# The attention result channel-major through DRAM, with the copies out issued by ScalarE, in a transformer layer on one Trainium2 core

## The reference

```python
# x: (32, 512, 256) float32
def attn(x):                                  # H = 16 heads, hd = 16
    q, k, v = split(x @ w_qkv.T + b_qkv)      # each (B, H, L, hd)
    scores = (q * hd**-0.5) @ k.T + mask      # mask: blocks of 128; block 0 is global
    out = softmax(scores) @ v                 # (B, H, L, hd) -> (B, L, D)
    return out @ w_out.T + b_out
def ffn(x):
    return relu(x @ W1 + b1) @ W2 + b2        # 256 -> 1024 -> 256
x = x + layernorm(attn(layernorm(x)))
x = x + layernorm(ffn(layernorm(x)))
```

## Time and profile before

| quantity | value |
|---|---|
| median of three runs | 2048.34 us |
| the profiled execution, its own time | 2041.29 us |
| its span, first to last instruction | 2039.5 us |
| mean granted clock of TensorE | 0.978 of full speed |
| busy: PE, PEld, DVE, ACT, POOL | 94%, 77%, 74%, 69%, 36% of the span |
| DMA | 160.60 MB, 79 GB/s |

### The profile page before, as it was taken

The page is one execution under the profiler, slowest core; times in us unless marked ns, Lnnn a source line. Parts: engine busy times, 40 slices in busy tenths (PEclk is TensorE's granted clock), DMA queues, the critical chain, the costliest instruction groups (busy, mean ns, idle before and its releaser), DMA issues. The chain is left out here.

```text
span 2039.5 us, 71012 instructions
## 1 busy us (share of the span) xinstructions
PE 1926.4 (94%) x27904; PEld 1575.7 (77%) x27904; DVE 1511.4 (74%) x2913; ACT 1406.0 (69%) x2343; POOL 741.6 (36%) x910
## 2 busy tenths in 40 slices
PE   5789999999999999999999999999999999999985
PEld 3458888777878877888777788787788887778775
DVE  4687777787777778778777777777777777876731
ACT  1457767777776777776677777677777677776763
POOL 3113333334333334433343433333433333343343
PEclk7799999999999999999999999999999999999997
DMA  5333434433333433333343333343334344333200
GB/s 144 74 70 80 89 77 86 85 76 82 81 81 79 93 79 80 79 81 81 82 85 80 79 77 81 80 94 78 77 77 86 76 87 85 78 81 69 56 28 17
DMA packets 132815, 160.60 MB, mean 79 GB/s; under 512 B 29408, under 2 KB 82400, under 8 KB 132576
## 3 DMA queue, kind: packets, MB, share of 16 engines
q1 hardware_dynamic: 130544, 154.13, 35.7%
q10 hardware_dynamic: 2032, 2.69, 0.4%
HBM read 38.21 MB, written 17.83 MB: 27 GB/s over the span
## 5 line engine op out<-in xcount | busy, mean ns | idle before, releaser
L817 DVE TENSOR_REDUCE max_bias<-p_pair 128x4 f32<-128x1024 f32 (+1 forms) x640 | 772.8, 1222 | 262.0 <-PE p_pair L571 139.8
L742 ACT ACTIVATE probs<-p_pair 128x1024 f32<-128x1024 f32 x640 | 634.8, 1026 | 208.4 <-PE p_pair L568 127.6
L964 POOL TENSOR_TENSOR h_lo<-h_f,h_hi 128x512 fp32r<-128x512 f32 x256 | 329.7, 1288 | 507.5 <-ACT h_hi L774 507.5
L571 PE MATMUL p_pair<-stack 49*128 49x256 f32 (+1 forms) x3072 | 319.6, 306 | 39.5 <-DVE max_bias L817 22.7
L774 ACT ACTIVATE h_f<-p_pair,b_s 128x256 f32<-128x256 f32 x512 | 248.8, 486 | 133.1 <-PE p_pair L598 133.1
L571 PEld LDWEIGHTS p_pair<-stack 49*128 49x128 f32 (+1 forms) x3072 | 226.9, 188 | 126.7 <-DVE max_bias L817 59.8
L598 PE MATMUL p_pair<-w_hi,h_hi 64*128 64x256 f32 x2048 | 309.4, 279 | 5.0 <-ACT h_hi L774 2.5
L598 PE MATMUL p_pair<-x_hi,w_hi 64*128 64x256 f32 (+1 forms) x2560 | 302.1, 306 | 9.6 <-DVE x_lo L827 5.2
L598 PE MATMUL p_pair<-w_hi,h_lo 64*128 64x256 f32 x2048 | 305.7, 275 | 0.0
L598 PE MATMUL p_pair<-w_lo,h_hi 64*128 64x256 f32 x2048 | 305.5, 275 | 0.0
L598 PE MATMUL p_pair<-x_hi,w_lo 64*128 64x256 f32 (+1 forms) x2560 | 297.7, 302 | 0.0
(11 more groups left out here) (81 smaller groups left out, 2792.9 us busy)
## 6 DMA issues: line engine op xcount, KB each, us to landing
stack<-qk SPq DMA_DIRECT2D x1536, 64.0 KB, 2.3
xr<-x SPq DMA_DIRECT2D x32, 512.0 KB, 4.2
out<-yf SPq DMA_DIRECT2D x64, 256.0 KB, 2.2
xa<-x SPq DMA_DIRECT2D x31, 512.0 KB, 3.8
shift_rows<-max_t SPq DMA_DIRECT2D x128, 8.0 KB, 1.4
stack<-shift_rows SPq DMA_DIRECT2D x128, 8.0 KB
probs<-w_qkv_t SPq DMA_DIRECT2D x2, 384.0 KB, 5.5
ya<-w ACTq DMA_DIRECT2D x1, 512.0 KB, 8.2
```

The costliest lines, as they stand in the source:

```text
L571: last = nc.tensor.matmul(dst[:, j, col:col + HALF].rearrange("p (a n) -> p a n", a=2), stack[r, stationary, at, kb * P:(kb + 1) * P], two ...
L742: nc.scalar.activation(probs[:, prob_slot(quad, c), :, :], banks("scores", n)[:, :, :], ACT.Exp, scale=SCALE).then_inc(exp_done, 1)
L817: nc.vector.tensor_reduce(dst, src, axis=AX.X, op=ALU.max, negate=True).then_inc(red_done, 1)
L964: nc.gpsimd.tensor_tensor(h_parts[1][:, m:m + 2, :], h_f[:, n % 2, :, :], h_parts[0][:, m:m + 2, :].bitcast(F32), ALU.subtract).then_inc(h ...
```

## The change

The attention result stays channel-major. Steps `o_t` and `o2` are taken out of TensorE's list. In their place:

- `read_o` copies the quad to SBUF as before, into one of two buffers.
- `store_o` (new, ScalarE, once for each quad) issues two DMAs: one moves the four rows of denominators from SBUF to the SBUF tile `den_q` (each row of 512 cut into 32 pieces of 16 elements, 64 bytes), the other writes all 128 partitions of 2 KB to DRAM (`o_rows`, 256 KB).
- SyncE gets six DMAs more for each batch: `load_o` twice (from `o_rows` to `o_ch`, 128 partitions of 2 KB), `store_inv` twice (inverted denominators to DRAM, 16 KB), `load_inv` twice (back, each row read 16 times, 256 KB).
- VectorE takes the reciprocals twice for each batch on a tile of 128 x 32 (`inverse`), multiplies twice on 128 x 512 (`normal_o`) and writes `o2_lo` in two halves; ScalarE writes `o2_hi` in two halves, all from SBUF.
- `o_ch` is the memory of `ya`, the tile of the output projection, so `load_o` waits until the sum of the batch before (`x1_done`) has read `ya`.
- The rows of the output weights are reordered on the host to the new order of channels.
- All tables of the order are written anew, and with them the assignment of PSUM pairs.

```diff
-        ("o_t", 0, -2, 0), ... ("o_t", 3, -2, 1), ... ("o2", 0, -2, 3)       (TensorE: gone)
+        ("exp", 12, -2), ("store_o", 1, -2), ("exp", 13, -2),                (ScalarE)
+        ("load_o", 0, -3), ("load_inv", 0, -3), ("store_inv", 1, -3),        (SyncE)
+        o_t = sb("o_t", [P, 2, L])
+        inv_b = sb("inv_b", [P, KD, L])
+        o_rows = nc.dram_tensor("o_rows", [KD, H // 2, 32, L], F32, kind="Internal").ap()
+        inv_rows = nc.dram_tensor("inv_rows", [KD, H // 2, L], F32, kind="Internal").ap()
+        o_ch = ya[:, :, :].rearrange("p (c a) n -> p c (a n)", c=KD)
...
+                elif what == "load_o":
+                    other, added = count(sp, b, 32, 16 * (n + 1)), count(sp, b, 2, 0)
+                    wait(sp, o_out[0], b, 32, 16 * (n + 1))
+                    reached(sp, o_out[1], other)
+                    reached(sp, x1_done, added)
+                    sp.dma_start(o_ch[:, n, :], o_rows[n, :, 0:HD, :].rearrange("h c n -> c h n")).then_inc(o_in[n], 16)
+                elif what == "store_inv":
+                    rows_free = count(sp, b, 16, 0)
+                    wait(sp, inv_done, b, KD, n + 1)
+                    reached(sp, inv_in[n], rows_free)
+                    sp.dma_start(inv_rows[n].rearrange("(j h) (m t) -> (h m) j t", j=2, t=DT),
+                                 inv_q[:, n, :, :]).then_inc(inv_out[n], 16)
+                elif what == "load_inv":
+                    read = count(sp, b, KD, n + 1 - KD)
+                    wait(sp, inv_out[n], b, 16, 16)
+                    reached(sp, on_done, read)
+                    sp.dma_start(inv_b[:, n, :],
+                                 inv_rows[n].unsqueeze(0).broadcast_to([HD, H // 2, L])).then_inc(inv_in[n], 16)
...
-                elif what == "o2":
-                    wait(pe, ev["o_t"], b, QUADS, QUADS)
-                    last = transposed(dst, lambda r, m: o_n[r, m % KB, m // KB * P:(m // KB + 1) * P], KD * KB)
-                elif what == "o_t":
-                    wait(pe, ot_done, b, QUADS, n + 1)
-                    last = transposed(dst, lambda r, m: o_t[r, m * P:(m + 1) * P], KB)
...
                 elif what == "read_o":
                     wait(act, pv_mm, b, QUADS, n + 1)
-                    wait(act, mm["o_t"], b, QUADS, n)
-                    nc.scalar.activation(o_t[:, :], banks("pv", n)[:, 0, :], ACT.Copy).then_inc(ot_done, 1)
+                    for s in (den_in, o_out):
+                        wait(act, s[n % 2], b, 32, 16 * (n // 2))
+                    nc.scalar.activation(o_t[:, n % 2, :], banks("pv", n)[:, 0, :], ACT.Copy).then_inc(ot_done, 1)
+                elif what == "store_o":
+                    rows_free, den_free = count(act, b, 16, 0), count(act, b, KD, n // 2 + 1 - KD)
+                    wait(act, ot_done, b, QUADS, n + 1)
+                    reached(act, o_in[n // 2], rows_free)
+                    reached(act, inv_done, den_free)
+                    heads = slice(4 * (n % 2), 4 * (n % 2) + 4)
+                    act.dma_start(den_q[:, n // 2, n % 2, :],
+                                 o_t[HD:P:32, n % 2, :].rearrange("h (m t) -> h m t", t=DT)).then_inc(den_in[n % 2], 16)
+                    act.dma_start(o_rows[n // 2, heads].rearrange("h c n -> (h c) n"),
+                                 o_t[:, n % 2, :]).then_inc(o_out[n % 2], 16)
+                elif what == "o2_hi":
+                    wait(act, on_done, b, KD, n + 1)
+                    wait(act, mm["op"], b, 1, 0)
+                    nc.scalar.activation(o2_t[0][:, n, :], o_ch[:, n, :], ACT.Copy).then_inc(hi_done["o2"], 1)
...
+                elif what == "inverse":
+                    for j in range(2):
+                        wait(dve, den_in[j], b, 32, 16 * (n + 1))
+                    wait(dve, inv_out[n], b, 16, 0)
+                    nc.vector.reciprocal(inv_q[:, n, :, :], den_q[:, n, :, :]).then_inc(inv_done, 1)
                 elif what == "normal_o":
-                    (reciprocal of den, two products into o_n, from PSUM)
+                    wait(dve, inv_in[n], b, 16, 16)
+                    wait(dve, o_in[n], b, 16, 16)
+                    nc.vector.tensor_tensor(o_ch[:, n, :], o_ch[:, n, :], inv_b[:, n, :], ALU.mult).then_inc(on_done, 1)
```

539 lines of the change are left out of this document (280 added, 259 removed), and 23 rows, old and new, of tables (LAST, ORDER).

## The result

The changed kernel takes 2126.6 us (median of four runs, 2121.4 to 2129.0), the kernel before 2048.4 in the same runs: the ratio is 1.038, with an interval of 1.035 to 1.040. The profiled execution of the changed kernel took 2129.0 us, its span is 2127.2.

What follows compares the result with a forecast made beforehand. TensorE's list, its steps in a row and short waits for PSUM pairs, was taken as the bound. Per batch -1.1 - 0.7 + 0.5 + 0.2 = -1.1 us, -35 us in 32 batches, plus 2 at the end: 2015 us, range 1984 to 2056.

Steps and rivals of the forecast that it cites:

- (a): TensorE's o_t and o2 transposes go: 1.1 us a batch gained, one o_t not counted because TensorE waits there anyway.
- (b): Five PSUM pair uses a batch go, with the waits behind o_n (0.36 us a batch); counted at nothing.
- (c): Stretch from the last f2 product to quad 3's product on TensorE: 7.6 us against 8.3, a gain of 0.7.
- (d): On TensorE, x1 takes x2's PSUM pair soon after it and waits for x_lo: a loss of 0.5 us.
- (e): ScalarE's eight DMA issues a batch, 0.5 us each, hidden beside TensorE's work: cost nothing, 1.0 us if one pause shows.
- (f): VectorE's swapped steps about even; its waits for DMAs, inverse 0 the tightest, cost 0.2 us a batch, ends 0 and 3.4.
- (g): DMA traffic of 2.1 MB more a batch: DMA engines' share from 0.39 to about 0.55, SyncE's queue has room.
- The ends: Last batch's result goes through DRAM, about 10 us of latency beside the previous batch's feed-forward: 2 us added.
- wrong in kind: Sign: turn shrinks by less than 0.5 us with all transposes gone; then the steps between them set the pace.
- the rivals: ScalarE's pauses reach TensorE, 2077 us, chance 0.14; DRAM chain takes the gain, 2045, 0.18; more than the transposes, 1988, 0.18.

Runs made afterwards that it cites:

- b_few: Kernel before, each o_t step making 2 of its 8 transposes and o2 2 of its 16 (38 fewer a batch); 2063.3 us, ratio 1.009.
- a_fill1: Changed kernel with scores_max 6 to 10 made twice, 16 more products a batch between quads 2 and 3; 2087.9 us, ratio 1.021.
- a_seven: Changed kernel with scores 16 and its exp ahead of quad 2's product, scores_max 9 and 10 behind quad 3's; 2182.1 us, ratio 1.067.
- b_act_dma: Kernel before with eight more DMAs a batch issued by ScalarE, four of 8 KB and four of 256 KB; 2049.0 us, ratio 1.003.
- a_best2: Changed kernel with scores_max 6 to 10 made twice and steps around op reordered on VectorE, SyncE and ScalarE; 2054.3 us, ratio 1.006.
- b_few_but_one: Kernel before with 32 of 48 transposes a batch left out, keeping all eight of o_t 2 between quads 2 and 3; 2043.5 us, ratio 1.000.
- b_traffic: Kernel before with eight more 256 KB DMAs a batch, issued by SyncE behind each load_stack; 2118.2 us, ratio 1.035.

## Why the prediction was wrong

By its own steps, for each batch:

- **(a), transposes, -1.1 us: the mis-sized term, and the step that failed.** It took the transposes' time as free to go and reckoned that the one in the gap was worth nothing, "where TensorE waits anyway". It was worth the clock. Taking it out made the old order 0.6 us a batch slower by the medians and 1.1 by the profiled turns (b_few), and the whole fall cost 1.76 in the new one (a_fill1). What the other transposes bring was too high as well: nothing that can be told for 32 of them, where 0.9 were reckoned. In the new order no run puts back the work of the transposes alone; there the gap is also longer (step c). That their absence is enough rests on b_few and on a_seven.
- **(b), no gain from the pairs:** not tested apart. The wait for `o_n` is gone; those for other readers of pairs came in its place, as the step said.
- **(c), the stretch:** from `f2` to quad 2's product 0.57 us, as said (0.6). From quad 2 to quad 3 5.18 and not 4.69: the copy starts 0.27 us after the product for 0.14 before, the first `exp` 0.71 after the copy's start for 0.49, the fourth `exp` adds 0.92, and TensorE goes on 0.43 after the last for 0.26: 1.44 us more, where 0.95 were taken. With the product of quad 2 that makes 8.04 us for 8.31, a gain of 0.3 and not 0.7. The prediction watched this stretch's length to 0.1 us, and never asked what waiting there does to the product behind it.
- **(d), `x2` and `x1`:** 0.5 us was too dear. The row of `x_lo` is 4.0 us in 25 turns, 0.2 a turn.
- **(e), ScalarE:** 256 issues at 0.556 and 0.502 us, as said; their cost was taken as nothing and measured as 0.24 us a turn with the traffic, in the old order (b_act_dma). Small and inside the bounds.
- **(f), VectorE:** wrong in kind. The two differences of 128x512 were priced at 0.63 us by a copy on ScalarE of that size; alone they take 0.66, beside GpSimd 1.77. The bounds looked at DMA landings, not at the neighbour, and the same rows of before had no such pair. With the waits around it on ScalarE's `relu` and on `h_lo`, this is 61.27 - 60.17 = 1.1 us a turn (a_fill1 against a_best2, by order alone). The order changed on three engines at once, so the 1.1 is not divided between these waits; moving one `o_lo` by itself brought 0.22 to 0.42.
- **(g), traffic:** right. No wait on `stack`, its landing 2.4 us. The DMAs of 256 KB in the detour landed after 3.2 to 3.9 us where 2.2 and 2.3 were taken, that of 16 KB after 1.8, in slack that held.
- **The ends, +2 us:** 17.5. With the clock held and the order mended it is still 14 (a_best2). TensorE's waits for `max_bias` and for `h_lo` rise there in small rows (behind 1800 us that for `h_lo` from 2.3 to 8.0 us in the changed kernel); it was not taken apart further.

The sum against the runs: the prediction had -1.1 us a turn, the profiled executions +2.8, a difference of 3.9 (by the medians the kernel is 78 us slower and not 88, so some 0.3 us of it is scatter). Of it 1.8 us is the clock and 1.1 the place around `op`; each is shown by an edit that takes it away. The other 1.0, the turn of a_best2 against the 59.1 reckoned, is put down to gains of (a) and (c) that never came. For (a) b_few_but_one shows such a shortfall in the old order; how the 1.0 us divides stays open.

The prediction called itself wrong in kind if the turn shrank by less than 0.5 us although all transposes were gone. It grew by 2.8, and the reason given for that case, that the steps between set the pace, leaves the clock out as well. None of the rivals had the clock either. All of them took TensorE's products at one speed. Of the two rules of the Trainium skill that the prediction weighed, the one on busy time (Trainium Kernel Development and Optimization, Performance Expectations) pointed the right way: the share of the weight loads said that there was room, and taking work away brought little. But its measure would not have told of the loss. The other (DMA: Bandwidth & Descriptors, Issuing engines are not separate DMA queues) did not come to bear: the stores on ScalarE hardly slowed `stack` (2.4 us for 2.3), and where traffic cost something, in b_traffic, it was issued in the list of the loads themselves. A third one was not weighed and should have been. The Trainium skill (TensorE: Matmul & The Clock Gate, A second HAM failure mode: psum-queue depth-cycling) tells of a kernel that cycles through its PSUM banks and pauses so often and so briefly between groups of products that the clock swings between its two levels. The trace agrees: the longest wait in the gap of that turn was 0.52 us, and the waits are several.

## What to carry to other kernels

Where a kernel's clock stands at full and its busiest stretch of waits is short of falling, work that "hides in a wait" may be what holds the clock: look at the granted clock behind each stretch of waits, in short stretches of the windows view, and price the products after it at both levels. If it falls, some harmless products in the gap are a test that takes one line, and here they paid 39 us (33 by the ratios).

Price a VectorE step with two SBUF operands twice, alone and beside GpSimd, and read from the timeline which it will be. And when a step is moved forward in a hand-written order, ask first what it waits for: it takes everything behind it along into that wait.

## What the runs showed of the hardware that was not expected

- Six transposes of 64x64 in a gap of 3.7 us, 0.2 us of work, decide whether the clock goes from 1.00 to 0.50: 24 falls in 25 turns without them, 1 with them, each in one profiled execution.
- A fall lasts some 6 us in the changed kernel and some 5 in b_few, and its largest cost is in the products behind the gap: 32 products took 4.4 us for 2.3.
- A difference of 128x512 with both operands in SBUF takes 0.66 us on VectorE, and 1.77 beside the same kind of operation on GpSimd, which itself goes from 1.29 to 1.69.
- 256 KB stores issued by SyncE between short DMAs that are waited for cost 2.3 us a turn for 2.1 MB, issue time and nine falls of the clock included; half as many bytes issued by ScalarE cost 0.24.
